# DMA transposes on SyncE's queue in place of TensorE transposes for the normalised rows of a routing stage

## The reference

```
xn = layernorm(x)
s  = attention_and_mlp(xn)            # elu+1 linear attention over 16 heads, MLP 1024-4096-1024
S  = slot_init                        # 64 slots of 1024
ctx = concat([xn, mean(S)])
h  = gelu(ctx @ w1 + b1)              # 2048 -> 512
logits = (h @ w2 + b2) / (|tau| + 0.1)  # 512 -> 64
alpha = softmax over the top 8 of the 64 logits, zero elsewhere
slot_input = alpha^T @ xn, over all 8192 rows;  denom = sum of alpha
S_new = GRU(slot_input / denom, S), then attention among the slots
g  = silu((alpha @ slot_values) @ wo + bo)
out = x + s * g
```

## Time and profile before

| | us |
|---|---|
| median of 2 runs | 2461.47 |
| lowest and highest run | 2460.18, 2462.76 |
| profiled execution | 2464.49 |
| span of the profiled execution, slowest core (core 1) | 2462.9 |
| spans of the other cores | 2437.2 to 2458.2 |
| routing stage in it | about 95 to 727 |

### The profile page before, as it was taken

One profiled execution on the slowest core, in us unless ns is written; L12 is line 12 of the kernel. 1 busy time (PEld: TensorE's weight loads), 2 busy tenths in 40 slices (PEclk: granted clock), 3 DMA queues, 4 the chain that ended last, 5 costly groups with the idle time before them and its releaser, 6 DMA issues. The chain is left out here.

```text
span 2462.9 us, 18900 instructions; the slowest of 8 cores (2437.2 to 2462.9 us)
## 1 busy us (share of the span) xinstructions
PE 1230.9 (50%) x6308; PEld 569.6 (23%) x6308; DVE 533.8 (22%) x1213; ACT 503.1 (20%) x748; POOL 122.3 (5%) x139
## 2 busy tenths in 40 slices
PE   0142534435443322454644825722068688598596
PEld 0021212222221100122221322310033233243242
DVE  0223133232210120322323233220120220300102
ACT  0144333433330000010100200200041240430521
POOL 1000000000010001000000000002201101001000
PEclk9976667667675555676866957956579889799798
DMA  9301021111107524252252331337945918809347
GB/s 177 67 34 69 35 69 34 69 69 35 35 8 118 102 43 60 52 116 43 82 99 60 82 69 56 94 73 121 139 54 52 148 41 86 154 3 115 88 39 99
DMA packets 341425, 183.65 MB, mean 75 GB/s; under 512 B 305171, under 2 KB 309396, under 8 KB 341332
## 3 DMA queue, kind: packets, MB, share of 16 engines
q0 software_dynamic: 182144, 72.72, 26.1%
q1 hardware_dynamic: 159188, 109.74, 15.9%
HBM read 204.81 MB, written 33.56 MB: 97 GB/s over the span
## 5 line engine op out<-in xcount | busy, mean ns | idle before, releaser
L662 PE MATMUL pT<-cIDb,xnb 128*128 128x128 bf16 x512 | 64.3, 305 | 316.8 <-ACTq L191 229.3
L676 PE MATMUL pM<-xnTs,w1ab 128*128 128x512 bf16 x512 | 148.3, 458 | 24.8 <-ACTq L191 24.7
L1980 PE MATMUL pMa<-h2T,fcwb 128*128 128x512 bf16 x512 | 127.3, 394 | 19.5 <-ACTq L191 19.5
L1917 DVE TENSOR_TENSOR y1t<-pTf,y1t 128x512 f32<-128x512 f32 x32 | 22.1, 692 | 524.3 <-PE pTf L2011 524.3
L1997 PE MATMUL pPb<-g1F,pjcb 128*128 128x512 bf16 x512 | 121.5, 399 | 9.1 <-DMA pjcb<-pjw 9.0
L662 PEld LDWEIGHTS pT<-cIDb,xnb 128*128 128x128 bf16 x512 | 49.2, 137 | 331.1 <-issue 331.1
L1980 PE MATMUL pMb<-h2T,fcwb 128*128 128x512 bf16 x512 | 123.2, 384 | 0.0
L1997 PE MATMUL pPa<-g1F,pjcb 128*128 128x512 bf16 x512 | 114.8, 383 | 10.3 <-DMA pjcb<-pjw 5.6
L516 DVE BATCH_NORM_STATS2 ST<-xld 128x6 f32<-128x512 f32 x64 | 43.6, 681 | 326.4 <-ACTq L191 325.9
L1580 ACT ACT_TABLE_LOAD x4 | 5.1, 1283 | 510.7 <-PE pBig L1533 510.7
L1964 PE MATMUL pT0d<-cIDb,h2b 128*128 128x128 bf16 x128 | 16.2, 307 | 164.0 <-DVEq L191 103.0
(11 more groups left out here) (260 smaller groups left out, 1678.4 us busy)
## 6 DMA issues: line engine op xcount, KB each, us to landing
xld<-x8k SPq DMA_DIRECT2D x64, 512.0 KB, 6.9
pjcb<-pjw POOLq DMA_DIRECT2D x32, 1024.0 KB, 10.8
scr_qk<-tmb SPq DMA_DIRECT2D x16, 512.0 KB, 2.7
y1scr<-XN SPq DMA_DIRECT2D x4, 2048.0 KB, 6.8
fcwb<-fcw POOLq DMA_DIRECT2D x32, 256.0 KB, 21.3
y1t<-y1scr SPq DMA_DIRECT2D x4, 2048.0 KB, 11.3
xre<-x8k SPq DMA_DIRECT2D x16, 512.0 KB, 12.0
out<-xre SPq DMA_DIRECT2D x16, 512.0 KB, 3.7
```

Source lines behind the costliest of these rows:

```text
L662: i = t.transpose(pT0[:, cc * 128:(cc + 1) * 128], xb[:, cc * 128:(cc + 1) * 128], cIDb[:])
L676: i = t.matmul(dstp[:, 0:512], w1ab[:, cc * 512 + ch * 128: cc * 512 + (ch + 1) * 128], xnTs[:, cc * 512:(cc + 1) * 512], start=(cc == 0), ...
L1917: i = v.tensor_tensor(y1v(mt).rearrange("p (s w) -> p s w", s=4)[:, :, d * 128:(d + 1) * 128], pTf[:, :].rearrange("p (s w) -> p s w", s=4 ...
L1980: i = t.matmul(dstp[:, :], fcwb[:, m * 1024 + cc * 128: m * 1024 + (cc + 1) * 128], h2T[:, cc * 512:(cc + 1) * 512], start=(cc == 0), stop ...
```

## The change

The transposes move from TensorE to the DMA engines. For each subtile SyncE waits for its copy or apply, and issues eight DMA transposes of 128x128 bf16, from `xnb` in SBUF straight into `xnTs` in SBUF, 32 for a macro-tile and 512 in all. They share a new semaphore `sxt`. TensorE waits once for all 32 of a macro-tile (`xt_w(mt)`), where before it did the transposes and waited for the fourth eviction. ScalarE has no evictions any more. The loads of mt + 2 are issued on the same queue ahead of the transposes of mt. Since `xnTs` is one buffer, SyncE also waits until the matmuls of mt - 1 are done. The step counts shrink by four for each macro-tile on TensorE and ScalarE. The transposes of `ALPHA` through `pT0` for own tiles stay on TensorE, with another wait ahead of them.

```diff
-                    t_c += 9 + (0 if m == 0 else
+                    t_c += 5 + (0 if m == 0 else
...
+                xt0 = X['xt']
+                xt_w = lambda m: xt0 + 512 * (m + 1)
...
                     @blk.sync
                     def _(s):
-                        for m in range(2, N_MT):
-                            s.wait_ge(sdv, v_apply(m - 2, 3))
+                        for m in range(N_MT):
+                            if 2 <= m + 2 < N_MT:
+                                mw = m + 2
+                                s.wait_ge(sdv, v_apply(mw - 2, 3))
+                                for st in range(4):
+                                    r = mw * 512 + st * 128
+                                    dmx(s, xslot(mw, st),
+                                        x8k[r:r + 128, :],
+                                        sx[mw % 2], 'x%d' % (mw % 2))
+                            if m >= 1:
+                                s.wait_ge(spe, t_h(m - 1, 3))
                             for st in range(4):
-                                r = m * 512 + st * 128
-                                dmx(s, xslot(m, st), x8k[r:r + 128, :],
-                                    sx[m % 2], 'x%d' % (m % 2))
+                                if own_f(m):
+                                    s.wait_ge(sac, a_copy(m, st))
+                                else:
+                                    s.wait_ge(sdv, v_apply(m, st))
+                                xb = xnbs(m, st)
+                                for cc in range(8):
+                                    s.dma_start(
+                                        out=xnTs[:, cc * 512 + st * 128:
+                                                 cc * 512 + (st + 1) * 128],
+                                        in_=xb[:, cc * 128:(cc + 1) * 128],
+                                        transpose=True).then_inc(sxt, 16)
+                                    X['xt'] += 16
...
                             if own_f(mt):
-                                t.wait_ge(sac, a_evac(mt + 1, 3))
+                                if mt >= 1:
+                                    t.wait_ge(sac, a_alphat(mt - 1))
...
                             par = mt % 2
-                            for st in range(4):
-                                if own:
-                                    t.wait_ge(sac, a_copy(mt, st))
-                                else:
-                                    t.wait_ge(sdv, v_apply(mt, st))
-                                if st == 0:
-                                    if mt >= 1:
-                                        t.wait_ge(sac, a_evac(mt - 1, 3))
-                                    if mt >= 2 and own_f(mt - 2):
-                                        t.wait_ge(sac,
-                                                  a_alphat(mt - 2))
-                                else:
-                                    t.wait_ge(sac, a_evac(mt, st - 1))
-                                xb = xnbs(mt, st)
-                                i = None
-                                for cc in range(8):
-                                    i = t.transpose(
-                                        pT0[:, cc * 128:(cc + 1) * 128],
-                                        xb[:, cc * 128:(cc + 1) * 128],
-                                        cIDb[:])
-                                fin(i, spe, 'pe')
-                            t.wait_ge(sac, a_evac(mt, 3))
+                            t.wait_ge(sxt, xt_w(mt))
...
-                            for st in range(4):
-                                a.wait_ge(spe, t_transp(mt, st))
-                                i = a.activation(
-                                    chunked(xnTs, 8, 512)[
-                                        :, :, st * 128:(st + 1) * 128],
-                                    chunked(pT0, 8, 128),
-                                    AF.Identity)
-                                finv(a, sac, 'ac')
```

More of the change, by code:

```diff
@@ L148, in build_nc @@
         sfq = E(nc.semaphore("sfq"))
+        sxt = E(nc.semaphore("sxt"))
         sx = [sx0, sx1]; swc = [swc0, swc1]; sfc = [sfc0, sfc1]
@@ L155, in build_nc @@
                  ss=0, k0=0, k1=0, k2=0, k3=0, ob0=0, ob1=0, ob2=0, ob3=0, al0=0,
-                 al1=0, fq=0)
+                 al1=0, fq=0, xt=0)
         ALPHA = E(nc.sbuf_tensor("ALPHA", [128, 1024], BF16))
@@ L445, in build_nc @@
                             + (2 if m >= 1 else 0))
-                    t_c += 9 + (0 if m == 0 else
+                    t_c += 5 + (0 if m == 0 else
                                 1 + (1 if own_f(m - 1) else 0))
                     a_c += (1 + (0 if m == 0 else 1)
-                            + (4 if own_f(m) else 0) + 9
+                            + (4 if own_f(m) else 0) + 5
                             + (1 if m >= 1 and own_f(m - 1) else 0))
@@ L466, in v_tailB @@
                     return v_tailA(m) + 1
-                t_transp = lambda m, st: pe0 + TB[m] + st + 1
-                t_h = lambda m, ch: pe0 + TB[m] + 4 + ch + 1
-                t_logit = lambda m: pe0 + TB[m] + 9
+                t_h = lambda m, ch: pe0 + TB[m] + ch + 1
+                t_logit = lambda m: pe0 + TB[m] + 5
                 def t_si(m):
-                    return pe0 + (TB[m + 1] + 10 if m + 1 < N_MT
+                    return pe0 + (TB[m + 1] + 6 if m + 1 < N_MT
                                   else TB[N_MT] + 1)
-                t_alphat = lambda m: pe0 + TB[m + 1] + 11
+                t_alphat = lambda m: pe0 + TB[m + 1] + 7
                 aoff = lambda m: (1 + (0 if m == 0 else 1)
@@ L481, in build_nc @@
                                         + (0 if m == 0 else 1) + st + 1)
-                a_evac = lambda m, st: ac0 + AB[m] + aoff(m) + st + 1
-                a_gelu = lambda m, ch: ac0 + AB[m] + aoff(m) + 4 + ch + 1
-                a_log = lambda m: ac0 + AB[m] + aoff(m) + 9
+                a_gelu = lambda m, ch: ac0 + AB[m] + aoff(m) + ch + 1
+                a_log = lambda m: ac0 + AB[m] + aoff(m) + 5
                 a_alphat = lambda m: a_log(m + 1) + 1
+                xt0 = X['xt']
+                xt_w = lambda m: xt0 + 512 * (m + 1)
                 def a_exp(m):
```

## The result

The changed kernel takes 2946.2 us (median of 11 runs), the kernel before 2465.6 us in the same measurement (10 runs). The ratio is 1.195, with a 95% interval of 1.191 to 1.199: 20% slower, 481 us. The forecast was 2633 us, 171 us slower: the sign was right, and the size was short by a factor of 2.8. The time lies inside the range, in the part that belonged to the rival with dear issues, whose reason turned out wrong.

What follows compares the result with a forecast made beforehand. The stage was taken as a serial chain, bounded by the order of its work. Later matmul starts (+115 us in ten tiles, +30, +15.4, +11) summed to +171 on 2461.5, about 2633 us; range 2520 to 3100.

Steps and rivals of the forecast that it cites:

- the rival with dear issues: SyncE's small transposes each occupy the queue as long as the fourth load, 1.502 us; about 3083 us in all; chance 28%.
- what bounds the stage: Stage from 95 to 727 us: each step waits for the one before, across tiles; the replaced stretch is 14.1 us in mt 7.
- (b): Issue of one small transpose on SyncE's queue: 0.60 us each, 19.2 us for the 32 of a macro-tile.
- (a): Loads ahead on SyncE's queue: their four issues take 2.83 us, then 1.1 us more before the first transposes get in.
- (c): Landing of the last transpose of a macro-tile: 2.4 us behind the end of its issue.
- the clock: TensorE's longer idle time before the matmul burst costs nothing; a burst never reaching the higher level would add 82 us.
- held-up issues: Each small transpose occupies SyncE for 1.502 us, as the fourth load did; about 3083 us; chance 28%.
- One at a time: A small transpose starts only when the one before has landed, at least 2.4 us each; about 3555 us; chance 9%, anything above included.
- cheap: Issues of 0.336 us without hold-up on SyncE's queue; 2486 us, within 2% of no change; chance 10%.
- fast case: A small transpose costs SyncE only its 0.170 us share of a large one; about 2400 us; chance 3%.
- The rule that I had called the loudest against the change: Skill page's 1309 ns for a 128x128 DMA crossbar transpose, as a rate: 41.9 us for 32, about 2985 us.

## Why the prediction was right or wrong

**Right: what bounds the stage.** It is one serial chain over all tiles: each microsecond between applies and matmuls counted sixteen times. With the measured terms the forecast's own sum closes: ten tiles, 44.4 - 14.1 = +30.3, 303 us; mt 1 to 3, 40.6 + 1.7 from the first copy against 11.7, +30.6, 92 us; mt 0, 44.2 from the first load's issue against 10.1, +34.1, 34 us; mt 14 and 15, 42.4 against 16.2, +26.2, 52 us. Together 481 us, the difference of the medians. By this sum nothing else in the kernel moved, and the DMAs had no other price.

**Wrong: step (b), the issue of one small transpose.** I took 0.427 us from a plain load plus 1/32 of a large transpose, 0.60 us. It is 1.232 us, 1.27 with the gap to the next. Two errors are in this step. The fixed part was taken from another kind of instruction: a plain copy of 512 KB costs SP 0.43 us, a transpose of even 16 KB costs 1.23. And the large transpose was read as a sum of 32 shares with hardly anything fixed in it. It can't tell a fixed part: the rows held one size only, and a line through one point has any slope. The half, single, fourfold and eightfold blocks, at 1.228, 1.232, 1.230 and 1.286 us (1.252 with the loads behind), show that the fixed part is all there is in this range. The term was mis-sized by (40.7 - 19.2) = 21.5 us a tile, 344 us in sixteen.

**Wrong, but small: (a) and (c).** The 1.1 us of hold-up behind the loads didn't occur: the four loads took 1.77 us instead of 2.83 and the transposes' pitch is the same from the first. The landing trails the last issue by 2.3 - 1.23 = 1.1 us, not 2.4, and the matmuls start 1.7 us behind the end of the last issue. So the hold-up is 1.1 us less, the loads' issues 1.1 and the end 2.4 - 1.7 = 0.7: together 2.9 us a tile in the ten tiles with loads, the other way than (b), and about 0.7 in the rest: some 33 us. 171 + 344 - 33 = 482.

**Right: the clock.** The granted clock still rises in the burst: it is 0.50 in 661 to 662, 4 to 5 us behind the start, and 0.91 in the window behind it. In the kernel before it is 0.50 in 412 to 413, 3 to 4 us behind the start, and 1.00 in 414 to 415. The burst takes 9.4 us in both, so the longer idle time cost nothing there, as forecast.

**The rivals.** The measured time lies near "held-up issues", but that wasn't the mechanism. That the range held the time is luck: its upper part came from the price of a load that was held up, and no transpose is held up in this kernel. The transposes of mt 14 and 15, which have no loads ahead, cost the same. The row has the last nineteen of mt 14 and the first of mt 15:

```profile
L520 SPq DMA_TRANSPOSE xnTs<-xnb x20: 1095/1232/1238, 1104.5 to 1145.4; - x20
```

"One at a time" is out as well: a block lands 2.3 us behind the start of its issue, and the pitch is 1.27. In mt 7 the first three land 4.5 to 6.5 us behind it, with the loads in flight, and SP still issues them in 1.16 to 1.23 us each. So these issues don't wait for what is in flight. The cheap and the fast case needed issues of 0.34 and 0.19 us. The rule that I had called the loudest against the change (the Trainium skill, VectorE: DVE Perf Modes, The three transpose paths, 1309 ns) agrees with the trace within 3%: the measured pitch is 1271 ns, and the estimate from it, 2985 us, was nearer than mine. I had set it behind a price built from rows of other instructions. It would have been the better choice to ask which of the two speaks of this instruction at this size. What the runs add is that the price is that of the issue, not of the block.

## What to carry to other kernels

On a queue, count the instructions before the bytes: here 32 issues of 32 KB cost 41 us, and the same megabyte in four issues cost 5.3 us. To price an instruction from another size, ask for two sizes; with one, keep the whole of it as a possible fixed part. And when a change removes a wait by the way, try to remove that wait in the old kernel first: here reordering alone gave all that the best measured form of the change gave.

## What the runs showed of the hardware

- A DMA transpose costs SP 1.23 to 1.29 us from 64x128 up to 128x1024 bf16 (medians of four sizes), 1.232 us for 128x128 both from SBUF and from HBM, and 4.83 us for 128x4096. A plain DMA of 512 KB costs 0.43 us.
- Small transposes behind 2 MB of loads in flight are issued at the same pace (1.27 us), though the first land late (up to 6.5 us in mt 7 instead of 2.3). Wide ones (256 KB each) are held up: 8.7 to 10.1 us for four instead of 5.3.
- 1 MB transposed from SBUF to SBUF in one piece lands 6.7 us behind the start of its issue, at 217 GB/s in between.
